# Graph layer on one core: where the slots are filled in a step, and how far ahead ranks, places and keys run

## Chip, cores and metric

One core of a Trainium2 chip runs the program. The metric is the device time of one execution in microseconds, the median of the runs shown.

## What is computed

A graph layer with residual and normalisation, on 12500 nodes of 32 features and 400000 edges sorted by their target `dst`:

```python
msg = jax.nn.relu(node_inputs[src] + edge_inputs)
agg = jax.ops.segment_sum(msg, dst, num_segments=N_NODES)
h = (1.0 + eps[0]) * node_inputs + agg
return h @ W.T + b
...
x = _layernorm(x + _L0_gnn_ref(x, edge_attr_32, src, dst, L0_gnn_W, L0_gnn_b, L0_gnn_eps), axis=-1)
```

## The kernel before

**Tiling.** The edges are cut into batches of 1920, 128 partitions by 15 tiles. The first batch is short (5 tiles); 208 full ones (`ROWS`) follow. In a full batch the rows `x[src]` of 7 tiles are gathered from HBM by indirect DMAs that POOL issues (`gather`, L552, 7 a batch). Those of the other 8 tiles (1024 edges) are looked up by matmuls in a copy of x that stands in SBUF as three bf16 parts.

**The look-up.** A source node has a bucket (32 of them) and a place in it. DVE marks the buckets of a batch's edges (`mark_buckets`, `ob`). PE counts, with matmuls on a triangle and on ones, how many edges of the same bucket came before (`count_ranks`, bank `ranks`). From that DVE makes the rank in the bucket (`count_before`, `find_rank`), the product of mark and place (`place_sources`, `placed`), the one-hot of the rank (`give_slots`, `in_slot`) and the key (`give_key`). PE multiplies `placed` with `in_slot` in 8 small matmuls (`fill_slots`, L1224): 32 buckets by 57 slots, each with its node's place. ACT copies them to SBUF (`copy_slots`, L973); SP writes them to HBM and reads them back spread over 128 partitions (`spread_slots`), and does the same with the keys. With one-hots of the slots (two thirds by DVE, one by ACT through a squaring and a relu, `square_slots` and `mark_slots`) PE fetches the nodes bucket by bucket: `look_in_buckets` (L1150), 96 matmuls with a weight load each, into four banks `l1`. ACT casts these into `table` (`fill_table`). With one-hots of the keys (`mark_keys`: three by DVE, one by ACT) PE picks from the table: `look_in_table` (L1169), four times 24 matmuls. DVE copies the picked rows into `rows_all` (`pick`, four a step).

**The sums.** DVE adds edge features and rows (`add_rows`), ACT takes the relu, DVE marks the target nodes relative to the batch's first (`mark_batch`), PE sums by node (`sum_batch`, 30 matmuls into the bank `win`), DVE adds that to the aggregate (`add_window`).

**Order.** Everything runs in steps s. Each engine goes through its part of a step in an order written out by hand in its `step`, and waits on semaphores. On PE: buckets of row s, node sums of batch s-1, table looks 0 and 1 of row s, slots of row s+2, table look 2, counts of row s+3, table look 3. On DVE: `mark_keys` 0 and 1 (s), four picks (s-1), `count_before` and `place_sources` (s+2), `add_rows` (s), `find_rank` and `give_key` (s+2), `mark_buckets` (s+3), `give_slots` (s+2), `pair_buckets` (s+3), `mark_keys` 2 (s), slot marks (s+1), `mark_batch` (s), sides, `add_window` twice. On ACT: key squaring, two table casts, key marks, relu, `square_slots` (s+1), `copy_slots` (s+2), `mark_slots` (s+1). POOL gathers for batch s+3 in three turns of 3, 2 and 2 tiles: the first waits for the whole bucket look (`l1_ready`), the second for table look 1 and the third for table look 3 (`blocks_looked`).

`placed`, `in_slot`, `ob`, `pairs` and `counts` are one buffer each; `slots` and `key` have two, `keys` and the copies in HBM four. `slot_ps` (32 by 57) stands in the bank of the ranks, where DVE also reads the numbers `rank_iota`; `win_iota` stands in the bank of the node sums.

## Time and profile before

| | |
|---|---|
| median of 3 runs | 2930.49 us (2925.21 to 2933.01) |
| the profiled execution | 2931.13 us |
| its span | 2929.0 us |
| mean granted clock of TensorE | 0.909 of full |
| busy share of the span | PE 81%, PEld 63%, DVE 62%, ACT 56%, POOL 49% |
| DMA | 81 GB/s |

PE is the matmuls, PEld the weight loads, which overlap them. Matmuls are pipelined and their ends are modelled. In a group of the page, busy time and mean length of one stand behind the first bar; behind the second stands the engine's idle time just before these instructions, with what ended most of it ("issue": nothing that the profile shows). In a timeline the bracket at the end is the idle time before the row. Times in windows and timelines are microseconds from the span's start.

### The profile page before, as it was taken

How to read it: one execution, taken by the hardware profiler on the slowest of the kernel's cores; microseconds unless marked ns; L12 is line 12 of the kernel's file. 1: busy time of each engine (PE TensorE's matmuls, PEld its weight loads, DVE VectorE, ACT ScalarE, POOL GpSimd, SP SyncE). 2: the span in 40 equal slices, each digit the busy share in tenths (PEclk: the TensorE clock that was granted, in tenths of full speed). 3: DMA queues.
4: the chain of work that ended last, by engine and by line, in shares of the span. 5: the costliest groups of instructions: out<-in, count | busy, mean ns of one | idle time of the engine just before them, and what ended most of it. 6: DMA issues, size and time to landing. Idle time of an engine off the chain costs nothing. (4 is left out here: it accounts for less than half of the span.)

```text
span 2929.0 us, 110879 instructions
## 1 busy us (share of the span) xinstructions
PE 2382.3 (81%) x49112; PEld 1842.9 (63%) x35800; DVE 1812.9 (62%) x4504; ACT 1635.8 (56%) x1720; POOL 1434.8 (49%) x1467
## 2 busy tenths in 40 slices
PE   4788888888888888788888888888887878888788
PEld 2566666666666666666666666666666666666664
DVE  5766666666666666665665656666666566565665
ACT  4655555555555555555555555555555555555554
POOL 4454545544545454455455445445555545545541
PEclk9988999989989899989999999898899999898988
DMA  5333333333333333333333333333333333333332
GB/s 123 68 86 79 81 81 79 86 76 78 86 77 81 83 76 83 81 79 85 78 78 86 79 76 86 76 84 81 78 86 79 79 82 79 86 79 76 86 79 50
DMA packets 244832, 236.54 MB, mean 81 GB/s; under 512 B 107748, under 2 KB 190750, under 8 KB 244805
## 3 DMA queue, kind: packets, MB, share of 16 engines
q1 hardware_dynamic: 198053, 212.15, 31.1%
q0 software_dynamic: 46752, 24.03, 5.8%
q8 instruction: 17, 0.28, 0.0%
q14 instruction: 10, 0.08, 0.0%
HBM read 233.21 MB, written 2.78 MB: 81 GB/s over the span
## 5 line engine op out<-in xcount | busy, mean ns | idle before, releaser
L550 POOL DMA_INDIRECT rows_all<-in_x,index x1461 | 1434.3, 982 | 1442.6 <-PE l L1162 611.9
L1144 PE MATMUL found<-table,oh 128*128 128x128 bf16 x13312 | 1288.3, 227 | 12.7 <-issue 11.9
L1184 PE MATMUL found<-table,oh 128*128 128x128 bf16 x6656 | 1271.7, 233 | 21.2 <-issue 12.8
L1184 PEld LDWEIGHTS found<-table,oh 128*128 128x128 bf16 x6656 | 928.3, 139 | 335.8 <-issue 122.5
L1162 PE MATMUL l<-xparts,oh 128*57 128x96 bf16 x19968 | 717.0, 225 | 434.3 <-issue 434.2
L1162 PEld LDWEIGHTS l<-xparts,oh 128*57 128x57 bf16 x19968 | 590.8, 121 | 560.0 <-issue 559.2
L798 DVE COPY_PREDICATED rows_all<-mask,found 128x256 f32<-128x256 uint16 x832 | 370.3, 445 | 657.5 <-PE found L1144 507.0
L971 ACT CAST table<-l 128x768 bf16<-128x768 f32 x416 | 330.3, 795 | 661.7 <-PE l L1162 632.4
L780 DVE TENSOR_SCALAR oh<-keys,lanes 128x1024 bf16<-128x1024 f16 x624 | 295.6, 489 | 190.9 <-PE found L1144 139.8
L1015 ACT ACTIVATE oh<-keys,minus_lanes 128x1024 bf16<-128x1024 f16 x208 | 238.9, 1148 | 264.6 <-PE found L1144 222.1
L996 ACT ACTIVATE oh<-slots,minus_lanes 128x1824 bf16<-128x1824 f16 x208 | 375.2, 1804 | 6.8 <-DMA slots<-slot_dram 6.8
L1003 ACT ACTIVATE oh<-oh 128x1824 bf16<-128x1824 bf16 x208 | 357.3, 1718 | 0.0
L768 DVE TENSOR_SCALAR oh<-slots,lanes 128x1824 bf16<-128x1824 f16 x416 | 277.7, 709 | 115.5 <-issue 75.2
L1021 ACT ACTIVATE oh<-oh 128x1024 bf16<-128x1024 bf16 x208 | 220.7, 1061 | 0.0
L1194 PE MATMUL win<-onehots,relus 128*32 128x40 f32 x6250 | 201.0, 225 | 21.9 <-issue 19.5
L1194 PEld LDWEIGHTS win<-onehots,relus 128*32 128x32 f32 x6250 | 173.7, 131 | 52.1 <-issue 30.1
L978 ACT CAST slot_row<-ranks 32x57 f16<-32x57 f32 x208 | 41.4, 199 | 293.4 <-PE ranks L1230 206.7
L813 DVE TENSOR_TENSOR onehots<-win,rel 128x600 f32<-128x600 f32 (+1 forms) x209 | 161.5, 773 | 5.9 <-PE win L1194 2.0
L810 DVE TENSOR_TENSOR msg<-rows_all,msg 128x480 f32<-128x480 f32 (+1 forms) x209 | 136.0, 651 | 0.1
L986 ACT ACTIVATE relus<-msg 128x480 f32<-128x480 f32 (+1 forms) x209 | 124.0, 593 | 16.3 <-DVE msg L810 16.3
L759 DVE TENSOR_TENSOR in_slot<-ranks,bucket 128x456 f16<-128x456 f32 x208 | 129.6, 623 | 0.0
L747 DVE TENSOR_TENSOR placed<-ob,src_sb 128x256 f16<-128x256 f16 x208 | 88.6, 426 | 41.8 <-DVE counts L731 22.7
(127 smaller groups left out, 1031.0 us busy)
## 6 DMA issues: line engine op xcount, KB each, us to landing
slots<-slot_dram SPq DMA_DIRECT2D x208, 456.0 KB
keys<-key_dram SPq DMA_DIRECT2D x208, 256.0 KB
msg<-in_edge SPq DMA_DIRECT2D x208, 128.0 KB
rows_all<-in_x,index POOLq DMA_INDIRECT x1461
msg<-in_edge SPq DMA_DIRECT2D x208, 112.0 KB
index<-in_src SPq DMA_DIRECT2D x208, 3.5 KB
key_dram<-key SPq DMA_DIRECT2D x208, 2.0 KB
slot_dram<-slot_row SPq DMA_DIRECT2D x208, 3.6 KB
```

What stands on the lines that cost most here:

```text
L550: pool.indirect_dma_start(to, None, x, bass.IndirectOffsetOnAxis(indices[:, j:j + 1], 0)).then_inc(done, 16)
L768: nc.vector.tensor_scalar(oh1[:, j, :], slots[:, two, :], lanes[:, j:j + 1], None, ALU.is_equal).then_inc(oh1_ready, 1)
L780: nc.vector.tensor_scalar(key_marks(b), by_edge(keys[:, four, :]), lanes[:, b:b + 1], None, ALU.is_equal).then_inc(oh2_ready, 1)
L798: nc.vector.copy_predicated(rows[slot][:, POOLED * D:ROW].rearrange("p (t f) -> p t f", f=D), mask[:, two, :, k:k + 1].bitcast(U16).to_bro ...
L971: nc.scalar.copy(table[:, some, :], l1_all[:, :].rearrange("p (k c) -> p k c", k=KEYS)[:, some, 0:PARTS * FOUND]).then_inc(table_ready, 1)
L996: nc.scalar.activation(oh1[:, DVE_SUBS, :], slots[:, two, :], ACT.Square, bias=minus_lanes[:, DVE_SUBS:DVE_SUBS + 1]).then_inc(slots_squar ...
L1003: nc.scalar.activation(at, at, ACT.Relu, scale=-2.0, bias=1.0).then_inc(oh1_act_ready, 1)
L1015: nc.scalar.activation(key_marks(b), by_edge(keys[:, four, :]), ACT.Square, bias=minus_lanes[:, b:b + 1]).then_inc(keys_squared, 1)
L1144: return nc.tensor.add_instruction(mybir.InstMatmult(name=nc.get_next_instruction_name(), engine=mybir.EngineType.PE, ldweights=False, ins ...
L1162: last = nc.tensor.matmul(l1_of(g)[half * HALF:half * HALF + CAP, :, :], oh1[:, j, b * CAP:(b + 1) * CAP], xparts[:, j * EVEN + b, :, :], ...
L1184: last = nc.tensor.matmul(to, key_marks(b)[:, :, t], part, start=begin, stop=end, skip_group_check=True)
L1194: last = nc.tensor.matmul(win_sums(g), relus[:, tiles[j], :], onehots[:, tiles[j], :], start=(j == 0), stop=(j == len(tiles) - 1))
```

## The change

`fill_slots` moves on PE from between table looks 1 and 2 to right behind the node sums, and its result from the bank `ranks` to the bank `win`. The work that leads to it runs one row further ahead: buckets, pairs and counts on row s+4, and ranks, places, one-hots of the ranks and keys on row s+3. `fill_slots` and `copy_slots` stay at row s+2. ACT copies the slots ahead of relu and squaring. `mark_batch` waits for that copy, as it reads from the bank `win`; `count_ranks` waits for `in_slot` instead of the copy. One more step is written out at the start, and the preparation that hung on the first steps keeps its place against row 0. SP writes and reads the keys of row s+3 where it wrote and read those of s+2.

```diff
     TURNS = [(0, 3), (3, 5), (5, POOLED)]
     EARLY, CHUNK = 8, 72
-    HEAD, FROM, TO = 4, -3, ROWS + 3
-    ROUNDS = (ROWS - 3 - HEAD) // RING
+    HEAD, FROM, TO = 4, -4, ROWS + 3
+    ROUNDS = (ROWS - 4 - HEAD) // RING
     TAIL = HEAD + ROUNDS * RING
...
         far_rows = rows_all[:, 0:ROW]
         rank_ps = ranks[:, 0:LOOK * BUCKETS].rearrange("p (t b) -> p t b", b=BUCKETS)
-        slot_ps = ranks[0:BUCKETS, 384:384 + CAP]
+        slot_ps = win[0:BUCKETS, 384:384 + CAP]
...
             def spread_keys(st):
-                if has(st, 2, ROWS):
-                    r, two, four = st.s + 2, slot_of(st, 2, 2), slot_of(st, 2, RING)
+                if has(st, 3, ROWS):
+                    r, two, four = st.s + 3, slot_of(st, 3, 2), slot_of(st, 3, RING)
                     sp.wait_ge(key_ready, r + 1)
                     sp.dma_start(key_dram[four].rearrange("(p t) -> p t", t=LOOK), key[:, two, :]).then_inc(key_written, 16)
+
+            def read_keys(st):
+                if has(st, 3, ROWS):
+                    r, four = st.s + 3, slot_of(st, 3, RING)
+                    sp.wait_ge(key_written, (r + 1) * 16)
+                    sp.dma_start(keys[:, four, :], key_dram[four:four + 1, :].to_broadcast([P, COLS])).then_inc(keys_loaded[four], 16)
             def spread_slots(st):
                 if has(st, 2, ROWS):
                     r, two, four = st.s + 2, slot_of(st, 2, 2), slot_of(st, 2, RING)
                     sp.wait_ge(slots_copied, r + 1)
                     sp.dma_start(slot_dram[four].rearrange("(b c) -> b c", c=CAP), slot_row[:, two, :]).then_inc(slots_written, 16)
-                    sp.wait_ge(key_written, (r + 1) * 16)
-                    sp.dma_start(keys[:, four, :], key_dram[four:four + 1, :].to_broadcast([P, COLS])).then_inc(keys_loaded[four], 16)
+                    read_keys(st)
                     sp.wait_ge(slots_written, (r + 1) * 16)
                     if isinstance(r, int) and r == 0:
                         sp.wait_ge(xparts_ready, 1)
                     sp.dma_start(slots[:, two, :], slot_dram[four:four + 1, :].to_broadcast([P, SLOTS])).then_inc(slots_loaded[two], 16)
+                else:
+                    read_keys(st)
             def step(st):
                 load_index(st)
                 spread_keys(st)
                 load_edges(st)
                 spread_slots(st)
-                if not st.inside and st.s == FROM + 2:
+                if not st.inside and st.s == FROM + 3:
...
                 for g in range(SPANS):
                     nc.vector.tensor_copy(base_row[:, g, 0:ROWS], win[0:1, g * ROWS:(g + 1) * ROWS])
-                own(nc.vector.tensor_copy(base_row[:, 0, ROWS:BATCHES], dst_first_sb[0:1, SHORT:SHORT + 1]))
+                nc.vector.tensor_copy(base_row[:, 0, ROWS:BATCHES], dst_first_sb[0:1, SHORT:SHORT + 1]).then_inc(bases_taken, 1)
+                dve.wait_ge(bases_taken, 1)
...
                 nc.vector.tensor_copy(far_flag[:, :], ranks[0:1, 0:1]).then_inc(flag_ready, 1)
             def mark_buckets(st):
-                if has(st, 3, ROWS):
-                    r = st.s + 3
+                if has(st, 4, ROWS):
+                    r = st.s + 4
                     wait_count(dve, products_ready, r)
                     nc.vector.tensor_tensor(ob[:, :, :], count_up(rank_iota, LOOK, BUCKETS), each(of_row(bucket, r), LOOK, BUCKETS),
                                             ALU.is_equal).then_inc(ob_ready, 1)
             def pair_buckets(st):
+                if has(st, 4, ROWS):
+                    dve.wait_ge(ob_ready, st.s + 5)
+                    nc.vector.tensor_tensor(pairs[:, :, :], ob[:, 0:LOOK - 2, :], ob[:, 1:LOOK - 1, :], ALU.add).then_inc(pairs_ready, 1)
+            def count_before(st):
                 if has(st, 3, ROWS):
-                    dve.wait_ge(ob_ready, st.s + 4)
-                    nc.vector.tensor_tensor(pairs[:, :, :], ob[:, 0:LOOK - 2, :], ob[:, 1:LOOK - 1, :], ALU.add).then_inc(pairs_ready, 1)
-            def count_before(st):
-                if has(st, 2, ROWS):
-                    r = st.s + 2
+                    r = st.s + 3
                     dve.wait_ge(ob_ready, r + 1)
                     dve.wait_ge(ranks_ready, r + 1)
                     nc.vector.tensor_tensor(counts[:, :, :], ob[:, :, :], rank_ps, ALU.mult).then_inc(counts_ready, 1)
             def find_rank(st):
-                if has(st, 2, ROWS):
-                    r = st.s + 2
+                if has(st, 3, ROWS):
+                    r = st.s + 3
                     with nc.allow_low_precision(reason="whole numbers up to 1024"):
                         nc.vector.tensor_reduce(of_row(bucket, r), counts[:, :, :], AX.X, ALU.add).then_inc(rank_ready, 1)
             def place_sources(st):
-                if has(st, 2, ROWS):
-                    r = st.s + 2
+                if has(st, 3, ROWS):
+                    r = st.s + 3
                     wait_count(dve, slots_ready, r)
                     dve.wait_ge(counts_ready, r + 1)
                     nc.vector.tensor_tensor(placed[:, :, :], ob[:, :, :], each(of_row(place, r), LOOK, BUCKETS), ALU.mult).then_inc(products_ready, 1)
             def give_key(st):
-                if has(st, 2, ROWS):
-                    r = st.s + 2
+                if has(st, 3, ROWS):
+                    r = st.s + 3
                     wait_count(dve, key_written, (r - 1) * 16)
                     dve.wait_ge(rank_ready, r + 1)
-                    nc.vector.tensor_tensor(key[:, slot_of(st, 2, 2), :], of_row(bucket, r), of_row(key_base, r), ALU.add).then_inc(key_ready, 1)
+                    nc.vector.tensor_tensor(key[:, slot_of(st, 3, 2), :], of_row(bucket, r), of_row(key_base, r), ALU.add).then_inc(key_ready, 1)
             def give_slots(st):
-                if has(st, 2, ROWS):
-                    r = st.s + 2
+                if has(st, 3, ROWS):
+                    r = st.s + 3
                     nc.vector.tensor_tensor(in_slot[:, :, :], count_up(rank_iota, LOOK, CAP), each(of_row(bucket, r), LOOK, CAP), ALU.is_equal).then_inc(placed_ready, 1)
             def mark_slots(st, j):
...
                     wait_count(dve, win_ready, m)
+                    if has(st, 2, ROWS):
+                        dve.wait_ge(slots_copied, st.s + 3)
                     mark(of_row(rel, row_of(m))[:, 0:n], n).then_inc(onehot_ready, 1)
...
                     turn_x()
                 mark_keys(st)
+                copy_slots(st)
                 relu(st)
                 square_slots(st)
-                copy_slots(st)
                 mark_slots(st)
-                if not st.inside and st.s == FROM + 1:
+                if not st.inside and st.s == FROM + 2:
                     round_x(1, x_mid)
...
             def count_ranks(st):
-                if has(st, 3, ROWS):
-                    r = st.s + 3
+                if has(st, 4, ROWS):
+                    r = st.s + 4
                     pe.wait_ge(ob_ready, r + 1)
                     wait_count(pe, counts_ready, r)
-                    wait_count(pe, slots_copied, r)
+                    if not (isinstance(r, int) and r <= 0):
+                        pe.wait_ge(placed_ready, r)
                     nc.tensor.matmul(rank_ps, before[:, :], ob[:, :, :], start=True, stop=False)
...
                     r = st.s + 2
                     pe.wait_ge(placed_ready, r + 1)
+                    if isinstance(r, int) and r == 2:
+
+                        pe.wait_ge(bases_taken, 1)
                     wait_count(pe, slots_copied, r)
...
                 if not st.inside and st.s == 1:
                     turn_x(st)
+                fill_slots(st)
                 look_in_table(st, 0)
                 look_in_table(st, 1)
-                fill_slots(st)
                 look_in_table(st, 2)
                 count_ranks(st)
                 look_in_table(st, 3)
-                if not st.inside and st.s == FROM + 1:
+                if not st.inside and st.s == FROM + 2:
                     place_kept()
```

## Rows read from the trace of the kernel before

**Rows 1.** One line's instructions, 100 to 2800 us: lengths, first and last start:

```profile
L1230 PE MATMUL ranks<-in_slot,placed x1584: 187/192/233, 105.1 to 2788.3; 128*32 128x57 f16 x198
```

**Rows 2.** The page: busy time of the engines, then two of its groups:

```profile
PE 2382.3 (81%) x49112; PEld 1842.9 (63%) x35800; DVE 1812.9 (62%) x4504; ACT 1635.8 (56%) x1720; POOL 1434.8 (49%) x1467
...
L1162 PE MATMUL l<-xparts,oh 128*57 128x96 bf16 x19968 | 717.0, 225 | 434.3 <-issue 434.2
...
L978 ACT CAST slot_row<-ranks 32x57 f16<-32x57 f32 x208 | 41.4, 199 | 293.4 <-PE ranks L1230 206.7
```

**Rows 3.** Windows of L1162 alone: start:end length, PE, PEld, PEclk, DMA, GB/s:

```profile
1512.36:1518.01 5.65, 3.27 (x96) 2.46 (x96) 1.00 0.42 132
1525.54:1532.33 6.79, 4.12 (x96) 3.46 (x96) 0.75 0.55 120
...
1553.74:1558.07 4.33, 2.89 (x96) 2.38 (x96) 1.00 0.37 119
1565.81:1572.33 6.52, 4.18 (x96) 3.40 (x96) 0.82 0.37 109
```

**Rows 4.** Windows, first microsecond of looks: PE, PEld, DVE, ACT, POOL, PEclk, DMA, GB/s:

```profile
1525.54:1526.54 1.00, 0.91 (x36) 0.77 (x34) 0.54 (x2) 0.84 (x1) 0.71 (x1) 1.00 0.91 179
1539.41:1540.41 1.00, 0.23 (x3) 0.21 (x2) 0.00 (x0) 0.00 (x0) 0.37 (x1) 1.00 0.69 164
1553.74:1554.74 1.00, 1.00 (x48) 1.00 (x48) 0.40 (x1) 0.56 (x1) 0.00 (x0) 1.00 1.01 373
```

**Rows 5.** Timeline of PE: start, length, what, count, idle before it:

```profile
1505.57 0.27 PE L1184 MATMUL found<-table,oh 128*128 128x128 bf16 x1
...
1508.42 0.41 PE L1230 MATMUL ranks<-in_slot,placed 128*32 128x57 f16 x8
1508.76 0.27 PE L1184 MATMUL found<-table,oh 128*128 128x128 bf16 x1
...
1510.55 0.27 PE L1215 MATMUL ranks<-ob,before 128*128 128x256 f16 x1 [0.23 <-ACT slot_row L978]
...
1512.36 0.95 PE L1162 MATMUL l<-xparts,oh 128*57 128x96 bf16 x35
...
1516.75 1.27 PE L1162 MATMUL l<-xparts,oh 128*57 128x96 bf16 x50 [0.49 <-issue]
1517.94 0.77 PE L1194 MATMUL win<-onehots,relus 128*32 128x40 f32 x30
```

**Rows 6.** Timeline of POOL, its gathers:

```profile
1508.51 0.95 POOL L550 DMA_INDIRECT rows_all<-in_x,index  x1 [0.31 <-issue]
...
1518.85 1.10 POOL L550 DMA_INDIRECT rows_all<-in_x,index  x1 [2.89 <-PE l L1162]
...
1521.52 0.95 POOL L550 DMA_INDIRECT rows_all<-in_x,index  x1 [0.30 <-issue]
1524.06 0.94 POOL L550 DMA_INDIRECT rows_all<-in_x,index  x1 [1.59 <-PE found L1144]
1525.31 0.94 POOL L550 DMA_INDIRECT rows_all<-in_x,index  x1 [0.30 <-issue]
```

**Rows 7.** Timeline of ACT, copy and mark of slots:

```profile
1510.21 0.20 ACT L978 CAST slot_row<-ranks 32x57 f16<-32x57 f32 x1 [1.44 <-PE ranks L1230]
1510.32 1.72 ACT L1003 ACTIVATE oh<-oh 128x1824 bf16<-128x1824 bf16 x1
...
1537.11 1.72 ACT L1003 ACTIVATE oh<-oh 128x1824 bf16<-128x1824 bf16 x1
```

**Rows 8.** Timeline of DVE, from `placed` to the slot marks:

```profile
1515.94 0.43 DVE L747 TENSOR_TENSOR placed<-ob,src_sb 128x256 f16<-128x256 f16 x1 [0.20 <-issue]
...
1518.65 0.48 DVE L780 TENSOR_SCALAR oh<-keys,lanes 128x1024 bf16<-128x1024 f16 x1
1519.58 1.42 DVE L768 TENSOR_SCALAR oh<-slots,lanes 128x1824 bf16<-128x1824 f16 x2 [0.45 <-issue]
```

**Rows 9.** Timeline of SP's queue, the slot DMA:

```profile
1511.83 0.32 SPq L506 DMA_DIRECT2D slots<-slot_dram  x1
```

## What the change will do: a prediction

> **What bounds the kernel now.** I read the page first: one execution takes 2931.1 us, of which 2929.0 are the span, so 2.1 lie around it. The page's chain is no help, since it shows the output stage alone. 208 steps of one pattern fill nearly all of the span; the fills of 198 of them start at 105.1 to 2788.3 [rows 1], so a step takes 2683.2 / 197 = 13.62 us. Of the page's groups one varies: the look in the buckets (L1162, 96 matmuls a step). It is busy 717.0 us and PE idles 434.3 us before its matmuls [rows 2]: 1151.3 / 208 = 5.5 us a step. No work of another engine ended the idle part ("issue").
>
> Windows laid exactly around this look show two forms: 4.33 us, and 5.65 to 6.79 [rows 3]. Of the twelve steps from 1512.36 on, four were short (3.6 to 4.4); four of the twelve are shown. The first microsecond of the look tells the forms apart [rows 4]: where POOL gathers nothing in it (0.00), PE starts 48 matmuls; where POOL is busy, PE starts 3 or 36. Long: 35 matmuls come at once and the last 50 at once, at 1516.75, and between them PE stands most of the time [rows 5]. Gathers at 1524.06 and 1525.31 run into the look that begins at 1525.54 [rows 6]. So I read: **a gather beside the start of the look costs it some 2 us; it is short when the second turn of gathers is over as it begins.** A page stands against this, SBUF — State Buffer of the Trainium skill, section Who interferes with whom: DMA never contends with a compute engine, and PE has ports of its own. By it the 434.3 us would have another cause, and the change might not reach them. The rows above show the coincidence, not what links the two.
>
> The gathers matter a second way. The last fill ends at 1508.42 + 0.41 = 1508.83 [rows 5], while a gather runs from 1508.51 to 1509.46 [rows 6]; ACT's copy of the slots, free by then and waiting for the fills alone, starts at 1510.21 [rows 7], 1.4 us late. The page has 293.4 / 208 = 1.4 us of such idle time a step [rows 2]. PE's signals are late while POOL gathers.
>
> **What the change removes.** (1) `count_ranks` no longer waits for ACT's copy. Two table looks took 1508.42 - 1505.57 = 2.85 us, one 1.42. The third begins at 1508.76 and so ends at 1510.18; the counts begin at 1510.55 [rows 5]. At most 0.37 us, and nothing where the copy was in time: I take 0.1. (2) ACT's copy moves ahead of relu and squaring, so the mark of slots (1.72 us) doesn't wait for it. It ended at 1512.04 [rows 7], 0.3 us before the look of 1512.36: just in time, so this is worth nothing by itself. (3) PE's work stays: 8 fills, 5 counts. SP issues the same DMAs, with key and slots for the same rows or one row further.
>
> **What the change adds: one wait.** `place_sources` of row s+3 waits for the fills of row s+2, which PE now makes in the same step, behind bucket look and node sums; before, they lay a step back. `placed` is one buffer, so the wait is real. DVE reaches it at 1515.94 [rows 8], 3.6 us after the look began. PE is through with the fills after: look 4.3 to 6.5, node sums 0.8 [rows 5] (I take 0.9, as some run at the lower level of the clock, 0.75 of full in the look of 1525.54 [rows 3]), fills 0.35: 5.6 to 7.8 us. DVE stands 2 to 4 us. It is busy 1812.9 us [rows 2], 8.7 a step, and has the room. Queued behind it on DVE: the add of the messages (ACT's relu waits for it), rank, key (SP's key DMA, and behind that on SP the edge loads and the slot DMA), `ob`, `in_slot`, `pairs`, the mark of key 2 (PE's table look 2 waits for it), the marks of the slots, the one-hots, the window adds.
>
> Late first is key 2. From the start of `placed` to the end of that mark it is 1518.65 + 0.48 - 1515.94 = 3.19 us [rows 8]; two signals add 0.1. PE comes to table look 2 2.85 us after the fills. It stands **0.45 us** a step, plus the lateness L of the fills' signal. The slot marks end at 1519.58 + 1.42, 1.9 us after key 2's [rows 8]; the bucket look needs them 3.5 us after it: hidden. ACT's relu, square and mark end some 5 us after the fills (square and mark are 1.8 and 1.72 of it), the next look begins 6.7 after them: hidden with 1.7 to spare. The slot DMA, issued at 1511.83 [rows 9], is read a step later; it goes out about 5 us after the fills, 1.5 us ahead of the look instead of 0.5: hidden. The one-hots' wait for ACT's copy and the counts' wait for `in_slot` are over 1 and 2.6 us after the fills, before they are reached: nothing. If these covers were gone, each microsecond would count in full, for PE waits for all of them. One more step written out at the start has compare, pairs and counts of row 0 alone: 0 if it lies beside the loading of x, 6 us if nothing covers it; I take 4.
>
> **L** decides. Beside the third gather L was 1.4. The new fills end 1.2 us after the bucket look, and the first gather of a turn starts 0.84 after it (1518.85 against 1518.01 [rows 3, 6]): their signal leaves within half a microsecond of a turn's start. Bounds: 0, as outside gathers, or below it nothing, since a signal can't come before its work; and 4.1, if it comes only 0.8 us after the turn's last gather, which ends at 1522.47 [rows 6]. Nearest is the node sums' end just before, which held up nobody. I take 0.4: many at 0, some at 2.
>
> **What comes back.** From one bucket look's end to the next one's start: sums 0.9, fills 0.35, `placed` to key 2 with signals 3.3, then table look 2, counts, table look 3, which took 1512.36 - 1508.76 = 3.6, less the 0.1 of (1): 8.05, with L 8.45. Before, it was 13.6 - 5.5 = 8.1. The second turn of gathers starts 6.05 us after a bucket look's end (1524.06 less 1518.01), and its two gathers take 2.2: over at 8.25, which is 0.2 us before the next look, where in long steps it ran 0.7 into it. So the short look (4.35) becomes the rule, 8.45 + 4.35 = **12.8 us** a step. Over 205 steps: 0.82 x 205 = 168; 2931.1 - 168 + 4 = 2767 us. The median of the runs is 0.6 below the profiled one; no correction.
>
> **Rivals.**
> **A**, the look is short where ACT's marks come early, and gathers don't matter. For it: the long look of 1512.36 has the marks 0.3 us before it. Against it: the marks of 1537.11 ended 0.6 us ahead of the look of 1539.41 [rows 7], which yet started 3 matmuls in its first microsecond, with a gather beside it [rows 4]. By A every look is short, and if L is 0 and PE's stand falls into pauses that it has anyway: 7.75 + 4.35 = 12.1; 2931 - 1.52 x 205 + 4 = 2623.
> **B**, the looks stay mixed (5.5): the second turn waits for table look 1, which ends 0.35 us later behind the fills, and moves along. 5.5 + 8.25 = 13.75; 2931 + 0.13 x 205 + 4 = 2962.
> **C**, slower: L stays what it was or grows. The fills sit in a turn of gathers, and now all of DVE's chain to key 2 hangs on their signal. Place: PE's stand before table look 2. Price: L a step; it decides from 8.05 + 4.35 + L = 13.62, L = 1.2 us. At L = 1.9: 14.3, 2931 + 0.68 x 205 + 4 = 3074. At the bound of 4.1: 16.5, 3525.
> **D**, nothing to be seen: the look gives back what the stand costs, 2925 to 2938.
>
> The first gather of a turn took 1.10 us, others 0.95 [rows 6]. The same section of SBUF — State Buffer says that GpSimd shares a port pair with VectorE, which locks it with two SBUF inputs or in its fast modes. The change puts DVE's adds and products under a turn's first gathers; by that rule the turns end later, and B and C weigh more. No term above uses it.
>
> **How the numbers follow.** Forecast 0.45 (2767, by itself 2690 to 2850), A 0.12, B 0.20, C 0.15, D 0.08. About 0.3%, 9 us, is what a measurement of this kernel can tell from no change. Faster: forecast, A, a fifth of B: 0.61. Within: D and a tenth of B: 0.10. Slower: C and the rest of B: 0.29. Low is 2640, which leaves out most of A; high 3020, which leaves out most of C.
>
> **What would show it.** DVE idle before `placed`, released by PE's fills, 2 to 4 us a step; the bucket look's idle time down from 434 towards 200 us; POOL at rest in the first microsecond of most looks; ACT's idle time before the slot copy under 0.5 us a step; PE idle before table look 2, released by DVE, of 0.45 + L. The prediction is wrong if that last one is over 1.6 us a step (then C), or if long looks stay the majority (then B).

## The result, and the profile after

The changed kernel takes 2946.56 us (median of 6 runs, 2936.73 to 2959.47), the kernel before beside it 2929.69 (2925.21 to 2933.01): ratio 1.0061, 95% interval 1.0036 to 1.0087. It is **0.6% slower**, where 2767 us (5.6% faster) was forecast. The profiled execution took 2948.88 us.

The page of the changed kernel: busy time of the engines, then groups (busy us, mean ns | idle us before them and its releaser):

```profile
PE 2291.3 (78%) x49112; PEld 1789.8 (61%) x35800; DVE 1800.0 (61%) x4504; ACT 1657.4 (56%) x1720; POOL 1434.6 (49%) x1467
...
L1195 PE MATMUL found<-table,oh 128*128 128x128 bf16 x6656 | 1249.0, 231 | 169.6 <-DVE oh L789 86.5
...
L1173 PE MATMUL l<-xparts,oh 128*57 128x96 bf16 x19968 | 693.3, 217 | 405.9 <-issue 402.2
...
L756 DVE TENSOR_TENSOR placed<-ob,src_sb 128x256 f16<-128x256 f16 x208 | 88.5, 426 | 715.0 <-PE win L1245 615.1
```

From the groups by line, the copy of the slots ("remote" is a signal whose sender the profile doesn't find):

```profile
L989 ACT CAST slot_row<-win 32x57 f16<-32x57 f32 x208 | 38.9, 187 | 58.7 <-PE win L1245 33.6 <-remote 25.2
```

L1173 answers to L1162 of [rows 2]: 1099.2 us instead of 1151.3, 5.28 us a step instead of 5.53. That is all that came back of the 1.2 us a step that was expected, and the rest of a step grew by more (table below). ACT's idle time before the copy fell from 293.4 to 58.7 us; DVE now waits for the fills (L1245), 715.0 us before `placed`; PE's idle time before the first matmul of a table look rose from 21.2 to 169.6 us.

Windows around four looks in buckets (L1173 alone) that answer to [rows 3]: length, PE, PEld, clock, DMA, GB/s. Then the first microsecond of three of them, as in [rows 4], with PE, PEld, DVE, ACT, POOL:

```profile
1490.94:1495.29 4.35, 2.88 (x96) 2.38 (x96) 1.00 0.35 103
1502.82:1509.21 6.39, 3.98 (x96) 3.05 (x96) 0.90 0.41 112
1518.11:1522.41 4.30, 2.82 (x96) 2.33 (x96) 1.00 0.56 170
1529.96:1536.16 6.20, 3.76 (x96) 2.91 (x96) 0.93 0.51 121
...
1502.82:1503.82 1.00, 1.00 (x33) 0.82 (x32) 0.56 (x2) 0.11 (x1) 0.98 (x1) 1.00 0.83 145
1518.11:1519.11 1.00, 1.00 (x50) 1.00 (x49) 0.97 (x3) 0.60 (x1) 0.00 (x0) 1.00 0.72 171
1529.96:1530.96 1.00, 1.00 (x34) 0.86 (x33) 0.43 (x2) 0.14 (x1) 0.85 (x1) 1.00 0.98 135
```

Short and long looks now take turns, and again POOL's column tells them apart. The timelines of POOL, PE and DVE over the same stretch (start, length, what, count, idle before it) show why:

```profile
1501.52 0.94 POOL L558 DMA_INDIRECT rows_all<-in_x,index  x1 [1.88 <-PE found L1155]
1502.77 1.04 POOL L558 DMA_INDIRECT rows_all<-in_x,index  x1 [0.30 <-issue]
...
1510.12 0.95 POOL L558 DMA_INDIRECT rows_all<-in_x,index  x1 [3.50 <-PE l L1173]
...
1515.49 1.35 POOL L558 DMA_INDIRECT rows_all<-in_x,index  x1 [1.93 <-PE found L1155]
1517.14 0.94 POOL L558 DMA_INDIRECT rows_all<-in_x,index  x1 [0.30 <-issue]
...
1523.24 0.95 POOL L558 DMA_INDIRECT rows_all<-in_x,index  x1 [1.82 <-PE l L1173]
...
1529.85 0.97 POOL L558 DMA_INDIRECT rows_all<-in_x,index  x1 [0.30 <-issue]
```

```profile
1502.82 1.03 PE L1173 MATMUL l<-xparts,oh 128*57 128x96 bf16 x31
1504.32 0.27 PE L1173 MATMUL l<-xparts,oh 128*57 128x96 bf16 x2 [0.47 <-issue]
1505.10 0.25 PE L1173 MATMUL l<-xparts,oh 128*57 128x96 bf16 x3 [0.51 <-issue]
...
1507.35 1.86 PE L1173 MATMUL l<-xparts,oh 128*57 128x96 bf16 x52 [0.47 <-issue]
...
1510.20 0.47 PE L1245 MATMUL win<-in_slot,placed 128*32 128x57 f16 x6
...
1514.88 0.27 PE L1195 MATMUL found<-table,oh 128*128 128x128 bf16 x1 [1.05 <-DVE oh L789]
...
1522.98 0.31 PE L1245 MATMUL win<-in_slot,placed 128*32 128x57 f16 x5
```

```profile
1511.56 0.43 DVE L756 TENSOR_TENSOR placed<-ob,src_sb 128x256 f16<-128x256 f16 x1 [5.18 <-PE win L1245]
...
1514.27 0.48 DVE L789 TENSOR_SCALAR oh<-keys,lanes 128x1024 bf16<-128x1024 f16 x1
...
1523.43 0.42 DVE L756 TENSOR_TENSOR placed<-ob,src_sb 128x256 f16<-128x256 f16 x1 [2.13 <-PE win L1245]
```

Behind the short look of 1518.11 the fills end at 1523.29, just as the gathers begin at 1523.24; DVE starts `placed` at 1523.43, so L, the time from the fills' end to DVE's start, is 0.14. The next look begins at 1529.96, 7.55 us behind the last one's end, while the second turn runs to 1529.85 + 0.97 = 1530.82, 0.86 into it: **long**. Behind the long look of 1502.82 sums and fills run slower and end at 1510.67, half a microsecond into the turn that began at 1510.12. Their signal reaches DVE at 1511.56, L = 0.89; PE stands 1.05 us before table look 2; the next look comes 8.90 us behind the last one's end, and the second turn, over at 1518.08, is just through: **short**. The short look makes the next signal prompt, and so the next look long.

This is the rule, not one pair of steps. Of 190 steps (8 to 197), 93 of the 94 behind a short look (under 5 us) had a prompt signal (L under 0.3 us), but only 35 of the 96 behind a long one. Behind the 128 prompt signals the next look was short in 27% of the steps, behind the 62 late ones in 97%. Over the same steps the timelines give:

| | before | after |
|---|---|---|
| period, mean | 13.64 | 13.71 |
| from a look's end to the next look, mean | 8.10 | 8.43 |
| L: median, 75%, 90% | | 0.14, 0.91, 1.58 (mean 0.50) |
| second turn's end, behind the look's start, mean | 0.37 | 0.38 |
| looks under 5 us | 39% | 49% |
| looks with that end at most 0.5 us in | 81, mean 4.26 | 69, mean 4.23 |
| the other looks | 109, mean 6.49 | 121, mean 5.88 |

So a step has a look that is 0.25 us shorter and a rest that is 0.33 us longer. The sum, 0.08 us over 205 steps, is 16 of the 18 us between the two profiled executions. The clock has a part in the looks too: short ones ran at the full granted clock in both kernels (1.00, 2.4 GHz), those of 5 us and more at 0.84 in the mean before and 0.90 after, as parts of them stood at the lower level (1.2 GHz). Those at full clock throughout still took 5.8 and 5.9 us, so the clock alone doesn't make a look long.

### The profile page after: what moved, and what is told of

It reads as the page before. It is cut to its first block and busy times, and to the rows that moved or that the text cites. A ratio compares the mean times of both kernels' runs of the same rounds, so it can differ in the third digit from the quotient of the medians.

```text
span 2946.7 us, 111533 instructions
## 1 busy us (share of the span) xinstructions
PE 2291.3 (78%) x49112; PEld 1789.8 (61%) x35800; DVE 1800.0 (61%) x4504; ACT 1657.4 (56%) x1720; POOL 1434.6 (49%) x1467
## 5 line engine op out<-in xcount | busy, mean ns | idle before, releaser
L1195 PE MATMUL found<-table,oh 128*128 128x128 bf16 x6656 | 1249.0, 231 | 169.6 <-DVE oh L789 86.5
L1155 PE MATMUL found<-table,oh 128*128 128x128 bf16 x13312 | 1260.6, 225 | 0.3 <-issue 0.3
L1173 PE MATMUL l<-xparts,oh 128*57 128x96 bf16 x19968 | 693.3, 217 | 405.9 <-issue 402.2
L1173 PEld LDWEIGHTS l<-xparts,oh 128*57 128x57 bf16 x19968 | 559.9, 115 | 539.3 <-issue 532.8
L756 DVE TENSOR_TENSOR placed<-ob,src_sb 128x256 f16<-128x256 f16 x208 | 88.5, 426 | 715.0 <-PE win L1245 615.1
L789 DVE TENSOR_SCALAR oh<-keys,lanes 128x1024 bf16<-128x1024 f16 x624 | 288.3, 490 | 9.5 <-PE found L1155 3.0
L1245 PE MATMUL win<-in_slot,placed 128*32 128x57 f16 x1664 | 91.7, 201 | 1.5 <-DVE base_row L700 1.1
```

The source lines that it names most:

```text
L789: nc.vector.tensor_scalar(key_marks(b), by_edge(keys[:, four, :]), lanes[:, b:b + 1], None, ALU.is_equal).then_inc(oh2_ready, 1)
L1155: return nc.tensor.add_instruction(mybir.InstMatmult(name=nc.get_next_instruction_name(), engine=mybir.EngineType.PE, ldweights=False, ins ...
L1173: last = nc.tensor.matmul(l1_of(g)[half * HALF:half * HALF + CAP, :, :], oh1[:, j, b * CAP:(b + 1) * CAP], xparts[:, j * EVEN + b, :, :], ...
L1195: last = nc.tensor.matmul(to, key_marks(b)[:, :, t], part, start=begin, stop=end, skip_group_check=True)
```

## The experiments

**Two conditions of the chip.** The same kernel before takes 2930, 2867, 2862 or 2913 us in four groups of runs, and 2166 us in two others, always within 0.6% of one value inside a group. In the groups near 2900 us PE **stutters** beside gathers: it stands, does a few matmuls and weight loads (mostly 3 to 8 together), and stands again, one such step in 0.70 to 0.77 us. In the groups of 2166 us it does not, with the same 1461 gathers (mean 961 ns in the changed kernel, 982 with the stutter). The packets of the gathers' DMA queue don't tell the conditions apart either: half of them took 44 ns or less in both. One chip number (2) occurs with either condition, 23 minutes apart, so it isn't a property of that chip alone. What sets it is open. The result above is with the stutter. Ratios below are to the kernel before in the same group, and each result names the condition. Microseconds compared across groups are less sure than ratios, as the groups with the stutter differ by 2.4% themselves. Theory G is the reading above: the second turn's end against the look's start makes the look short or long.

**No gathers (with the stutter).** One run each of both kernels, without the gathers and without DVE's and SP's waits for them; the gathered rows are left out of the output:

```
-                    sp.wait_ge(rows_gathered[slot], gathered(slot, use - 1))
+                    sp.wait_ge(index_loaded[slot], use * 16)
...
-                        for j in range(j0, min(j1, SHORT) if isinstance(b, int) and b == 0 else j1):
-                            gather_tile(rows[slot][:, j * D:(j + 1) * D], index[slot], j, rows_gathered[slot])
...
+            nc.vector.memset(rows_all[:, :], 0.0)
...
-                    dve.wait_ge(rows_gathered[slot], gathered(slot, use))
```

> The changed kernel without POOL's gathers in the loop (the rows of 7 tiles of each full batch are not fetched, a constant stands in their place, so its output is not the reference's). Theory G (gathers beside PE's work stretch the bucket look and hold PE's signals back): in the changed kernel the look idles 402 us by issue and takes 5.3 us a step on average, 4.3 or 6; without gathers every look should have one form with hardly any idle time, 2.2 to 2.6 us for 96 matmuls (82 of them came in 1.94 us before a gather began), DVE should start `placed` 0.1 us after the fills in every step, and a step should take about 2.4 + 7.5 = 9.9 us, so some 2100 us in all. Rival S (instruction supply or the sequencer's start sets the look): both forms stay, the look's idle time stays near 400 us and the time near 2900.

> The kernel before without POOL's gathers in the loop (the same rows left out, output not the reference's). Theory G: one form of look, 2.2 to 2.6 us; ACT copies the slots within 0.1 us of the fills instead of 1.4 us later. With no gathers the change's own cost is bare: DVE's chain behind the fills makes PE stand 0.45 us a step before table look 2, so this kernel should be some 0.3 to 0.45 us a step (60 to 90 us) faster than the changed one without gathers. Rival S: about 2900 us and two forms.

2144.9 us after, 2139.8 before, where the kernel before takes 2867. Groups by line, after and then before:

```profile
L1193 PE MATMUL found<-table,oh 128*128 128x128 bf16 x6656 | 1193.0, 226 | 139.8 <-DVE oh L788 129.5 <-DVE rows_all L806 10.2
...
L1171 PE MATMUL l<-xparts,oh 128*57 128x96 bf16 x19968 | 465.5, 207 | 2.3 <-ACT oh L1012 2.3
```

```profile
L1182 PE MATMUL found<-table,oh 128*128 128x128 bf16 x6656 | 1193.3, 226 | 61.1 <-DVE oh L779 34.3 <-DVE rows_all L797 9.5 <-ACT x_turned L960 0.4
...
L1160 PE MATMUL l<-xparts,oh 128*57 128x96 bf16 x19968 | 465.5, 207 | 1.6 <-ACT oh L1001 0.9 <-issue 0.7
```

All "issue" time of the look but 0.7 us is gone, and with its waits it takes (465.5 + 2.3) / 208 = 2.25 us a step. In this condition gathers, or the transfers that they start, are needed for the stutter. The change by itself trades evenly: PE waits 78.7 us more before table looks (139.8 - 61.1), and is busy 57.8 us less (1958.4 against 2016.2).

**Five gathers, then two (with the stutter).** The first turn takes five gathers, the second the last two, behind the next row's table looks:

```
-    TURNS = [(0, 3), (3, 5), (5, POOLED)]
+    TURNS = [(0, 5), (5, POOLED)]
...
-                            pool.wait_ge(blocks_looked, (b - RING + 1) * KEYS + k * KEYS // 2)
+                            pool.wait_ge(blocks_looked, (b - RING + 2) * KEYS)
```

> The changed kernel with POOL's turns of 3, 2, 2 gathers made 5 and 2: the middle turn doesn't wait for table look 1 any more. Theory G says that a look is long (about 6) when the second turn of gathers runs into it, as it does in the steps whose fills' signal was prompt (turn over 0.85 us after the look's start). Five gathers in a row end 7.1 us after a look's end, 0.4 to 0.5 us before the next look begins, so nearly all looks should be short (4.3): period 4.3 + 7.6 = 11.9 us in most steps, near 2600 us. Danger by the same theory: the fills' signal is as before, within the first turn. Rival (the long look follows from the half clock or from DMA traffic of slots and keys, not from the gathers): looks stay half long, 2900 to 2950 us.

> The kernel before with turns of 5 and 2. Theory G: the same shift of the look's form, most looks 4.3 instead of 6.5, 4.35 + 7.6 = 12 us a step, near 2600 us; but PE's signals are held back to the end of the longer turn (7.1 + 0.8 = 7.9 us after the look), so ACT's copy of the slots comes later than now (5.5) and the marks of slots end at 9.8, after the look could begin (7.6): then a step takes 9.8 + 0.3 + 4.3 = 14.4 us and the kernel is no faster, 2950 to 3050 us. The changed kernel, whose copy hangs on the early fills, should not suffer from this. Rival: as for e3, no change of forms.

After: 3080.82 us, ratio 1.0746 (1.0706 to 1.0785). Before: 3275.86, 1.1431 (1.1399 to 1.1462). The looks did as theory G says: 93 and 94% under 5 us, the turn's end 2.9 and 3.7 us ahead of them. Both times were missed, near 2600 us after and 2950 to 3050 before. The time went elsewhere. Groups of the changed kernel with this edit:

```profile
L1195 PE MATMUL found<-table,oh 128*128 128x128 bf16 x6656 | 1258.3, 232 | 161.7 <-issue 152.1 <-DVE rows_all L807 5.5 <-DVE oh L789 2.0
...
L1173 PE MATMUL l<-xparts,oh 128*57 128x96 bf16 x19968 | 645.1, 218 | 281.0 <-issue 280.6
...
L1227 PE MATMUL ranks<-ob,before 128*128 128x256 f16 x208 | 58.6, 282 | 124.5 <-issue 121.7 <-DVE in_slot L768 2.5 <-DVE ob L726 0.2
```

125 us of the look's idle time are gone, but the counts (L1227) now stand 124.5 us, and the stretch from table look 2 to the end of table look 3 grew from 3.4 to 5.7 us a step: the stutter hits the table looks and counts under the fifth gather. In the kernel before it is worse, as its fills lie there too: ACT's copy idles 777.9 us, and the counts, which wait for it, 350.6.

**The second turn let go earlier (with the stutter).** It is let go by a mark of DVE's instead of by table look 1 (after; before has `+ 1` behind the product):

```
-                            pool.wait_ge(blocks_looked, (b - RING + 1) * KEYS + k * KEYS // 2)
+                            if k == 1:
+                                pool.wait_ge(oh2_ready, (b - RING + 2) * DVE_KEYS)
+                            else:
+                                pool.wait_ge(blocks_looked, (b - RING + 1) * KEYS + k * KEYS // 2)
```

> The changed kernel with one wait of GpSimd's moved: the second turn of gathers (2 of 7) is let go by VectorE's mark of key 2 instead of by TensorE's second table look. In the profile of the changed kernel that mark ends at 1514.75 and the turn starts at 1515.49, so it should start some 0.7 us earlier. Theory G (the length of a look in buckets is set by where the second turn ends against the look's start; in steps with a prompt signal it ends 0.85 to 0.99 us inside the look, which is then long): it ends about 0.2 inside, the look is short (4.3 to 4.7 us) in over 80% of the steps, and the period is 12.0 to 12.8 us: 6 to 10% faster than the changed kernel, ratio to before 0.90 to 0.95. Rival P (TensorE's own order sets the look, the gathers only share the time): no change within 0.5%, ratio to before about 1.005. Rival M (the turn merges with the first one, gathers in a row hold TensorE's signals longer): as with five gathers in a row, the tail behind table look 2 grows to 4 us or more, ratio above 1.02.

> The kernel before with the same wait moved: the second turn is let go by VectorE's mark of key 0 of the next row (ends 1522.70 where the turn starts at 1524.06). Theory G: the turn starts 0.6 to 1.1 us earlier, its end moves from +0.4 us (mean) behind the next look's start to before it, looks become short (4.3 to 4.7 us where the mean is 5.53) in over 80% of the steps, and the period falls from 13.6 to 12.5 to 13.0: ratio 0.92 to 0.96. Rival P: ratio 1.00. Rival M: the signals of table looks 1 and 2 are held longer, ratio above 1.01.

After: 2986.39 us, ratio 1.0440 (1.0423 to 1.0458). Before: 2977.28, 1.0378 (1.0338 to 1.0417). By the time, rival M in both. In the changed kernel the turn starts 1.4 us earlier in the mean and 93% of the looks are short (mean 4.38), but the first and the second turn lie 0.6 us apart (1.7 in the changed kernel), and the stretch behind table look 2 takes 5.2 us instead of 3.4. In the kernel before the edit hardly moved the turn (start 6.08 us behind the look's end, for 6.27) and 46% of the looks were short where over 80% were expected, so that run tests theory G little; its stretch behind table look 2 grew from 3.7 to 4.3 us. The counts of the changed kernel with this edit:

```profile
L1236 PE MATMUL ranks<-pairs,ones 128*128 128x192 f16 (+2 forms) x624 | 93.7, 220 | 113.6 <-issue 113.6
```

So I read the pause between the turns as needed: PE recovers in it. No run varied the pause alone.

**Key 2 marked ahead of the wait (with the stutter).** In the changed kernel DVE's mark of key 2 moves ahead of `place_sources`, and so ahead of the new wait:

```
                 count_before(st)
+                for b in range(EARLY_KEYS, DVE_KEYS):
+                    mark_keys(st, b)
                 place_sources(st)
                 add_rows(st)
...
-                for b in range(EARLY_KEYS, DVE_KEYS):
-                    mark_keys(st, b)
```

> The changed kernel with VectorE's mark of key 2 moved ahead of the products, and so ahead of VectorE's wait for the fills' signal: TensorE no longer stands before table look 2, however late that signal comes. The prediction put that stand at 0.45 + L a step and took it for the main cost (rival C). Theory G: the stand goes (idle time before table look 2 from 170 us to under 40 us), the rest of a step becomes 7.6 us or less in nearly all steps instead of 7.55 and 8.3 to 9.2 in turns, the second turn of gathers then runs 0.5 to 1 us or more into nearly every look, under 20% of the looks are short, their mean grows from 5.28 to 5.9 to 6.3 us, and the time stays within 1% of the changed kernel: ratio to before 0.99 to 1.015. Rival C (the stand is what the change costs): the looks stay as they are, and the whole stand comes back: 0.6 to 0.8 us a step, ratio 0.95 to 0.965.

2875.86 us, ratio 1.0053 (1.0029 to 1.0077), as for the changed kernel itself. Its groups:

```profile
L1195 PE MATMUL found<-table,oh 128*128 128x128 bf16 x6656 | 1244.9, 231 | 14.7 <-issue 7.3 <-DVE rows_all L807 6.5
...
L1173 PE MATMUL l<-xparts,oh 128*57 128x96 bf16 x19968 | 706.8, 221 | 430.6 <-issue 410.5 <-ACT oh L1014 12.8 <-DVE oh L777 4.6
```

The stand is gone (169.6 to 14.7 us) and, by the ratios, gave nothing. The rest of a step fell from 8.43 to 7.96 us (7.6 expected), the look's mean went from 5.28 to 5.38 (5.9 to 6.3 expected), and the second turn ends 0.94 us into it in the mean (0.38 in the changed kernel). These two profiles come from groups in which the kernel before differs by 68 us (2930 and 2862), so where the stand's time went can't be balanced from them. Rival C falls: it expected 0.95 to 0.965. Theory G has the sign and the time, but not the size: 42% of the looks were still short where under 20% were expected.

**More work ahead of the look.** In either kernel n (3 or 6) wide matmuls of 384 columns, or 48 small ones of 96 (`l1_of(0)[0:CAP, :, :]` from `xparts[:, 0, :, :]`), whose results the look overwrites:

```
+                    wait_count(pe, table_ready, (r - 1) * 2 + 1)
+                    for _ in range(6):
+                        nc.tensor.matmul(l1[0][0:CAP, 0:SIDE * PARTS * D], oh1[:, 0, 0:CAP],
+                                         xparts[:, 0:SIDE, :, :], start=True, stop=True)
```

> The changed kernel with more work on TensorE: six matmuls of 384 columns ahead of each look in buckets, whose results the look overwrites. At full clock they take about 1 us a step, 0.96 us by 2304 columns at 2.4 GHz. Theory G: the look starts 1 us later against the second turn of gathers, which is then over (within 0.1 us) when it starts; the look is short in over 80% of the steps (4.3 to 4.7 us by the look's line), the period is 7.55 to 8.4 + 1.0 + 4.4 = 12.9 to 13.4 us: with the additional work the kernel is 1 to 5% faster than the changed one, ratio to before 0.96 to 1.00. Rival P (the gathers only take time in proportion): the work is added, 208 x 1.0 = 200 us, ratio 1.07.

> The changed kernel itself, as the reference for the runs beside it on this chip. Ratio to before 1.003 to 1.009; looks in buckets short (under 5 us) in about half of the steps.

> The changed kernel with three additional matmuls of 384 columns ahead of each look in buckets, about 0.5 to 0.6 us a step; six of them added 242 us of busy time and the kernel became only 0.6% slower than the changed one. Theory G: the steps with a prompt signal end at 7.55 + 0.55 = 8.1 us behind their look, the second turn of gathers then runs 0.3 to 0.45 us into the next look instead of 0.85 to 0.99, which was short in 98% of such steps: short looks in over 75% of the steps, period 12.7 to 13.3, ratio to before 0.96 to 0.995, so a version faster than both. Rival P (the gathers share time in proportion): 208 x 0.55 = 115 us more, ratio 1.045. Rival Q (the total is bound by what TensorE gets done while gathers run, whatever its order): no gain and no loss, ratio 1.003 to 1.012 as for none and for six.

> The changed kernel with 48 additional matmuls of 96 columns (and their 48 weight loads) ahead of each look: the same time on TensorE as the six wide ones (48 x 22 ns = 1.06 us at the look's free rate), but 96 instructions where those were 12. Theory F (gathers starve TensorE of instructions: in traces so far some 90 to 97 of its instructions run from the start of a long row of gathers until it begins to stutter, whether that takes 2.1 or 4.8 us, and then 3 to 8 per 0.73 us): the instructions have to be brought too, and they cost 1.5 us a step or more beyond the six wide ones: ratio to before 1.09 to 1.20. Rival G alone (only the delay counts): as with the six wide ones, ratio 1.01 to 1.02.

> The kernel before with the six wide matmuls (1.17 us busy a step by the profile of that edit on the changed kernel). Theory G: the next look starts at 8.1 + 1.1 us behind the last one's end, the second turn (mean end +0.4 us before) is over, the looks are short in over 80% of the steps (1 us less in the mean), and the time stays within 1.5% of before: ratio 0.995 to 1.015. Rival P: 208 x 1.17 = 243 us more, ratio 1.085.

The last four of these, and the next four, met the condition without the stutter; the two after them met the stutter again.

> The changed kernel itself, as the reference beside the next three. If this chip shows the stutter of TensorE under gathers (before 2860 us or more): ratio to before 1.003 to 1.009, looks short in about half of the steps. If it doesn't (before near 2166 us, looks of 2.2 us in all steps): ratio 1.000.

> Three additional wide matmuls (384 columns) ahead of each look in the changed kernel. With the stutter, theory G: the next look starts 0.5 us later, the second turn's end moves from 0.85 to 0.99 us into the look to 0.35 to 0.5, short looks in over 70% of the steps, ratio to before 0.96 to 1.00. Rival Q (what TensorE gets done while gathers run sets the total, whatever the order): 1.003 to 1.012, no better than with none and with six. Rival P (they cost their time in proportion): 1.03 and more. Without the stutter: 1.030, as measured there.

> 48 additional small matmuls (96 instructions with their weight loads, 1.06 us at the look's free rate) ahead of each look in the changed kernel. With the stutter, theory F (TensorE is short of instructions while gathers run: some 90 to 97 from the start of a long row of gathers, then 3 to 8 per 0.73 us): they cost more than the 1.81 us a step (377 us in all) that they cost on the chip without it, 2.5 us a step or more, ratio to before 1.18 or more. Rival G alone (only time and delay count): less than there, as the delay shortens the looks, as it did for the six wide ones: ratio 1.01 to 1.10. Without the stutter: 1.174.

> Six additional wide matmuls ahead of each look in the kernel before. With the stutter, theory G: the looks, 5.53 us in the mean, become short (about 4.5 us) in over 80% of the steps, ratio to before 0.995 to 1.02. Rival P: 1.085. Without the stutter: 1.028.

> Three additional wide matmuls (384 columns) ahead of each look in the changed kernel. With the stutter (before 2860 us or more), theory G: the second turn's end moves from 0.85 to 0.99 us into the look to 0.35 to 0.5, short looks in over 70% of the steps, ratio to before 0.96 to 1.00. Rival Q (what TensorE gets done while gathers run sets the total, whatever the order): 1.003 to 1.012. Rival P: 1.03 and more. Without the stutter: 1.030.

> 48 additional small matmuls (96 instructions with their weight loads, 1.06 us at the look's free rate) ahead of each look in the changed kernel. With the stutter, theory F (TensorE is short of instructions while gathers run): 2.5 us a step or more, ratio to before 1.18 or more. Rival G alone: 1.01 to 1.10. Without the stutter: 1.174.

| ratio to before | with the stutter | without it, twice |
|---|---|---|
| changed kernel | 1.0061 (1.0036 to 1.0087) | 1.0002 and 1.0004 (0.9992 to 1.0014) |
| three wide, after | 1.0193 (1.0142 to 1.0245) | 1.0297 and 1.0304 |
| six wide, after | 1.0121 (1.0056 to 1.0186) | not run |
| six wide, before | not run | 1.0277 and 1.0282 |
| 48 small, after | 1.1073 (1.1028 to 1.1119) | 1.1736 and 1.1742 |

With the stutter, six wide matmuls (242.4 us busy) cost 0.6% beyond the changed kernel, 17 us. The two intervals overlap, so that is anything from nothing to about 1.3%, and rival P's 7% is out. Taking from each look the free time of its wide matmuls (0.16 us each), the look itself falls from 5.28 to 4.58 us in the mean and is under 5 us in 81% of the steps; the second turn ends 0.35 us ahead of it. That is theory G's mechanism, but its ratio was missed (0.96 to 1.00 expected). Three wide ones refute its threshold (about half a microsecond into the look): the turn's end moved from 0.86 to 0.43 us (median), as planned, and still 42% of the looks were short, with a mean of 5.24; they cost 38 us, which refutes rival Q's 1.003 to 1.012 and rival P's 1.03 too. Without the stutter the wide ones cost less than their time as well: six add 60 us to the kernel before, where 6 x 0.16 us a step would be 200; three add 65 to the changed one. Of the looks with that end at most 0.5 us in, 90% were short in the kernel before and 100% in the changed one, but 52% here (153 looks).

The 48 small ones told nothing between instructions and time. They were sized by the look's free rate of 22 ns each, but take twice as long. A likely reason, untested: the look's matmuls write to the lower and the upper half of the partitions in turns (`half` in `look_in_buckets`), the 48 to the lower half alone. The timeline without the stutter, first the small ones, then the look:

```profile
1403.75 2.14 PE L1168 MATMUL l<-xparts,oh 128*57 128x96 bf16 x46
...
1405.80 2.22 PE L1177 MATMUL l<-xparts,oh 128*57 128x96 bf16 x94
```

2.14 us for 46. They cost 1.81 us a step without the stutter (377 / 208) and 1.42 with it (294 / 208); there the look's own 96 matmuls take 3.3 us in the mean for 5.3, so the delay gives part back. Theory F (TensorE short of instructions) expected 1.18 and more, and its number fails. The theory itself stays untested: the page counts 17 packets and 0.28 MB on the instruction queue q8 in either condition, for 111533 instructions of the changed kernel, and so doesn't show a difference in how instructions arrive. What links gathers and stutter stays open.

Without the stutter the change makes **no difference**. There is no profile of the kernel before alone in this condition; the changed kernel has: two windows around looks, with PE, PEld, DVE, ACT, POOL, clock, DMA, GB/s; the timeline of PE; then groups by line:

```profile
1099.36:1101.60 2.24, 2.24 (x101) 2.12 (x98) 1.92 (x5) 1.95 (x2) 1.00 (x2) 1.00 0.84 173
1109.34:1111.57 2.23, 2.23 (x102) 2.16 (x102) 1.89 (x5) 1.88 (x2) 1.05 (x2) 1.00 0.81 181
```

```profile
1106.12 0.27 PE L1195 MATMUL found<-table,oh 128*128 128x128 bf16 x1 [0.71 <-DVE oh L789]
...
1109.34 2.23 PE L1173 MATMUL l<-xparts,oh 128*57 128x96 bf16 x96
```

```profile
L1195 PE MATMUL found<-table,oh 128*128 128x128 bf16 x6656 | 1193.9, 226 | 153.7 <-DVE oh L789 138.7 <-DVE rows_all L807 10.1 <-ACT table L982 0.2
...
L756 DVE TENSOR_TENSOR placed<-ob,src_sb 128x256 f16<-128x256 f16 x208 | 93.4, 449 | 48.8 <-DVE counts L740 38.4 <-PE win L1245 9.6 <-issue 0.2
```

A look with a whole microsecond of gathers beside it takes 2.23 us, as in the run without gathers. And 1461 gathers cost almost nothing: 2166 us against 2140 or 2145 without them, in different groups of runs.

## Why the prediction was wrong, step by step

- **The step that failed** is the end of the second turn: the sum 6.05 + 2.2 = 8.25 us, and with it "0.2 us before the next look, so the short look becomes the rule". Measured are 8.81 us, 0.38 inside the look. The bullets follow the prediction's order; this one is taken apart below.
- **What bounds the kernel**: half right. The looks' idle time goes with the gathers: without gathers 2.3 us of it are left. The reading "short when the second turn is over as the look begins" holds in the profiles of before and after (90 and 100% of the looks with its end at most 0.5 us in are short, 0 and 21% of the others). Moving the turn ahead made 93% of the looks short, and six wide matmuls 81%; three did not. The prediction said that it had coincidence, not the link; that link shows only in one condition of the chip. SBUF — State Buffer of the Trainium skill, section Who interferes with whom (DMA never contends with a compute engine), is borne out by the runs without the stutter, 2.23 us with gathers beside. In the others PE idles beside gathers, 434.3 us before the looks of the kernel before, by a cause that is open.
- **The removed wait, and ACT's copy**: right. PE's idle time before the counts fell from 22.5 to 10.6 us, 0.06 us a step for the 0.1 taken; the copy's own idle time fell by 235 us to 0.28 us a step (under 0.5 forecast), and nothing came of it, as forecast.
- **The added wait**: DVE stands 715.0 / 208 = 3.4 us a step, 2 to 4 forecast. PE's stand before table look 2, 0.45 + L: without the stutter, where DVE comes to `placed` 0.29 us behind the fills, 138.7 / 208 = 0.67 for 0.74. With the stutter it is at most 169.6 / 208 = 0.82, forecast 0.85; the profile puts 86.5 of the 169.6 us down to DVE's mark and 76.4 to "issue", but with the mark moved 14.7 are left in all. The chain behind it was costed well.
- **L**: 0.50 in the mean, 0.4 forecast; 75% of the signals within 0.91.
- **The rest of a step**: 8.43 us, forecast 8.45. As a mean right, but with luck: no common step has that length. Behind a prompt signal the median is 7.54 us, where the terms without L add up to 8.05; behind a late one it is 8.93.
- **The second turn over at 8.25 us**: this step failed. It ends at 8.43 + 0.38 = 8.81 in the mean, 0.56 later. Of that, 0.22 is that the 6.05 us to its start was one case of the kernel before, where the mean was 6.27. Another 0.23 is that the start moved to 6.50, which the sum left out. Table look 1, which lets the turn go, ends only 0.07 us later, with 0.35 us of fills ahead of it (4.24 to 4.31 us behind the look's end); the rest of the 0.23 lies between that end and POOL's start (2.04 to 2.19). The last 0.11 is the turn itself, 2.31 us for 2.2: some first gathers are longer, 1.35 us at 1515.49 instead of 0.95. Over all turns gathers did not get longer, 982 ns in the mean in both kernels, so DVE's adds and products under them, which the prediction weighed last, added nothing to their total.
- **"So the short look becomes the rule"**: failed twice. By that 8.81 the turn ends inside the look, not before it. And two means (8.45 and 8.25) were compared where the rest has two forms, about 7.55 behind most prompt signals and 8.3 to 9.6 behind most late ones. The prompt ones, the majority, bring the long look. What looked like a cost (L) is what makes a short look possible, and the wanted short look makes L small again.
- **Rival B** came out in what it said is seen: looks mixed, long ones just the majority (96 of 190), the second turn later, 2962 us for 2946.6. Its number is near in part by luck: it took the look at 5.5 us (5.28 measured) and the rest at 8.25 (8.43), where the forecast had 8.45 for that same rest. Its chance of 0.20 was too low: the fills' 0.35 us ahead of table look 1 were booked on PE's path in the forecast, and not on the turn that this look lets go. Rival A falls with the runs without gathers; C with the key mark moved. D's "nothing to be seen" is what the runs without the stutter gave, but not for its reason: the look takes 2.23 us there and has nothing to give back.

With the stutter, nothing that keeps all the work was faster than the kernel before. Six orders of the same work (the changed kernel and five edits of order) lie 0.5 to 14% above it. Where the looks gained most, table looks and counts lost more.

## What to carry to other kernels

Where a quantity decides by a threshold, compare its values step by step, not its mean. List the two or three forms that a step takes, with what each makes of the next one, before a gain is booked on "becomes the rule". An idle group marked "issue" that vanishes with a neighbour's DMA work is worth a run without that work, and a second one in another group of runs: a quarter of this kernel's time hung on a condition that no edit touches. A stall that moves when it is pushed (five gathers first, the turn earlier) is not won until the whole step is shorter.

## What the runs showed of the hardware

- The kernel before takes 2166 us in one condition and 2862 to 2930 us in the other, and the profiled runs of all kernels that gather have granted clocks of 0.99 in the one and 0.91 to 0.98 in the other; within a group of runs it never changed. Which one holds can't be read from the program.
- In the second, beside gathers PE goes on in steps of 0.70 to 0.77 us with mostly 3 to 8 matmuls and loads each, and is free again 0.5 to 1.1 us behind a turn's last gather. From the start of four or five gathers in a row it came through some 88 to 100 matmuls and loads before its first such step (the median of most kernels with over ten such rows), whether that took 1.4 or 4.8 us. Behind the start of two in a row the median was 52 to 57 in nine of ten kernels, 0.6 to 0.7 us in, but single rows vary widely.
- There, in the changed kernel, all 51 signals of the fills that left in the first 0.1 us of a turn reached DVE after 0.13 to 0.14 us; the 37 that left 0.5 to 0.8 us into it took 0.86 to 1.68.
- The time at the lower level of TensorE's clock fell from 535 us in the kernel before to 390 in the changed one and the mean granted clock rose from 0.909 to 0.934, while the profiled time rose by 18 us.
